# Merging order of a middle image's side steps: deadlines of one pace, or each with a correction of its own

## What is computed

```
x = x + conv3x3(gn(x))                          # layer 0
h = relu(bn1(nin(gn(x))))                       # layer 1, the dear one
y = mean over 4 directions d of mamba(h in direction d)
x = x + relu(bn2(nin2(y + h)))
x = x + gn(x) * gates(row and column means, two small mambas of 32 tokens)   # layer 2
x = x + post(circuit of 4 qubits(pre(gn(x))))   # layer 3
```

## Time and profile before

| | |
|---|---|
| median of 3 runs | 15168.12 us (15164.93 to 15168.78) |
| profiled execution | 15170.1 us, its span 15168.0 us |
| instructions | 190881 |
| granted TensorE clock, mean | 0.895 |
| PE, PEld busy | 85%, 54% |
| DVE, ACT, POOL busy | 89%, 61%, 90% |
| HBM | 207 GB/s over the span |

### The profile page before, as it was taken

The page is one execution under the profiler, slowest core; times in us unless marked ns, Lnnn a source line. Parts: engine busy times, 40 slices in busy tenths (PEclk is TensorE's granted clock), DMA queues, the critical chain, the costliest instruction groups (busy, mean ns, idle before and its releaser), DMA issues.

```text
span 15168.0 us, 190881 instructions
## 1 busy us (share of the span) xinstructions
PE 12942.3 (85%) x60700; PEld 8148.5 (54%) x60700; DVE 13545.8 (89%) x9901; ACT 9178.0 (61%) x10559; POOL 13633.9 (90%) x4234
## 2 busy tenths in 40 slices
PE   7888888888888888888888888888888888888886
PEld 4555555555555555555555555555555555555554
DVE  6988998889898898988899888999989899898996
ACT  4655665656666665665566665665656666566663
POOL 6998999989999898998989998999989899898996
PEclk8998998889899888989889998889988889888997
DMA  4655555555555555555555555555555555555653
GB/s 173 231 214 209 210 217 218 216 206 211 211 220 218 209 213 207 222 219 210 209 210 216 220 212 211 211 212 219 220 205 214 207 219 219 211 211 205 222 221 131
DMA packets 582385, 3200.85 MB, mean 211 GB/s; under 512 B 65875, under 2 KB 65883, under 8 KB 319075
## 3 DMA queue, kind: packets, MB, share of 16 engines
q1 hardware_dynamic: 581346, 3187.69, 56.6%
HBM read 3107.73 MB, written 29.36 MB: 207 GB/s over the span
## 4 chain that ended last, share of the span: by engine, by line
POOL 27%; issue 25%; PE 24%; DVE 17%; ACT 5%; DMA 1%; DVEq 1%; POOLq 0%; ACTq 0%; SPq 0%
POOL ring L884 18%; PE work L1387 13%; POOL ring L867 9%; DVE ring L1375 9%; PE y_acc L1402 6%; DVE slot L1364 4%; PE slot L1387 2%; PE y_acc L1387 2%; ACT ring L1041 1%; ACT L900 1%; DMA b_rows<-cb_rows_scratch 1%; DVE du L1163 1%; ACT stack L940 1%; ACT stack L936 0%; ACT yz L966 0%
## 5 line engine op out<-in xcount | busy, mean ns | idle before, releaser
L884 POOL TENSOR_TENSOR ring<-ring,c_rows 128x2048 f32<-128x2048 f32 x2048 | 9282.8, 4536 | 997.8 <-DVE ring L1375 993.7
L1375 DVE TENSOR_TENSOR_SCAN ring<-ring,slot 128x1024 f32<-128x1024 f32 x2304 | 5263.6, 2285 | 261.6 <-ACT ring L1041 38.2
L1402 PEld LDWEIGHTS y_acc<-wk,ring 128*128 128x128 f32 x32768 | 4252.3, 155 | 1880.0 <-issue 1021.7
L1402 PE MATMUL y_acc<-wk,ring 128*128 128x128 f32 x32768 | 4762.4, 297 | 489.7 <-POOL ring L884 406.8
L867 POOL TENSOR_TENSOR ring<-du,b_rows 128x1024 f32<-128x1024 f32 x1792 | 4236.3, 2365 | 286.6 <-PE y_acc L1402 211.0
L1375 DVE TENSOR_TENSOR_SCAN ring<-slot,ring 128x1024 f32<-128x1024 f32 x1792 | 4074.2, 2274 | 192.1 <-POOL ring L867 116.5
L1041 ACT ACTIVATE slot<-dt,a_neg 128x1024 f32<-128x1024 f32 x1792 | 1997.6, 1115 | 2784.0 <-DVE ring L1375 2777.6
L1364 DVE TENSOR_TENSOR slot<-du,slot 128x1024 f32<-128x1024 f32 x2304 | 2797.4, 1214 | 271.0 <-PE slot L1387 179.7
L1041 ACT ACTIVATE ring<-dt,a_neg 128x1024 f32<-128x1024 f32 x2304 | 2600.9, 1138 | 206.5 <-PE y_acc L1402 157.3
L1387 PE MATMUL work<-h_new,fused 128*128 128x512 f32 x4096 | 2160.0, 638 | 101.7 <-ACT dt L952 53.7
L1387 PE MATMUL slot<-stack,sel 96*128 96x512 bf16 x4608 | 1540.7, 419 | 719.4 <-DVE ring L1375 639.0
(11 more groups left out here) (173 smaller groups left out, 10050.2 us busy)
## 6 DMA issues: line engine op xcount, KB each, us to landing
c_rows<-cb_rows_scratch SPq DMA_DIRECT2D x2048, 1024.0 KB, 4.7
b_rows<-cb_rows_scratch SPq DMA_DIRECT2D x1792, 512.0 KB, 5.5
x_next<-in_x SPq DMA_DIRECT2D x32, 512.0 KB, 5.4
x_new<-x_next SPq DMA_DIRECT2D x32, 512.0 KB, 6.7
h_old<-h_new SPq DMA_DIRECT2D x32, 512.0 KB, 2.9
x_old<-x_new SPq DMA_DIRECT2D x32, 512.0 KB, 6.8
out<-x_old SPq DMA_DIRECT2D x32, 512.0 KB, 2.9
cb_rows_scratch<-stack SPq DMA_DIRECT2D x128, 96.0 KB
```

The costliest lines, as they stand in the source:

```text
L884: pool.tensor_tensor(pair, pair, c_rows[:, k % CB_BUFS, :, :], ALU.mult).then_inc(prod_ready, 1)
L1375: dve.tensor_tensor_scan(slot, a, b, 0.0, MUL, ADD).then_inc(scan_done, 1)
L1402: ins = pe.matmul(chunk(out_t, j), chunk(x, j), kc("ident"), is_transpose=True, start=start and j % (BANK // P) == 0, stop=stop, skip_grou ...
```

## The change

`lay` gets two arguments: the width of the window of choices, and a tuple of corrections for each stream. After the deadlines are worked out, each side step's due time is moved by half its correction, in us. For a middle image `image_plan` makes one plan only, with pace 3.22, a window of .2 and the table `SHIFTS`, six tuples with 160, 112, 44, 132, 12 and 19 whole numbers. The first and the last image are planned as before. The numbers of `SHIFTS` come from a search over the planner's timeline.

```
+PACE, WITHIN = 3.22, 0.2
+SHIFTS = [
+    (-230, -191, -308, 19, 76, 26, 91, -352, -323, -167, -317, 29, -260, -307, -343, 6, 629, 465, 26, -200, 249,
...
+    (234, -159, -25, -220, 215, -10, -88, 90, -220, -176, -61, 4, -296, -538, -351, -246, -773, -620, -647, -361,
...
+    (202, 74, 272, -168, -291, 21, -91, -294, -217, -279, -238, -551, -202, -15, 70, -208, -92, -254, 68, -551, -801,
...
+    (-98, -35, -51, 11, 209, 231, 79, 130, 240, -367, 126, -117, -215, -98, 6, 116, 4, -156, 233, -30, -30, -221,
...
+    (-56, -584, -160, -103, -67, -323, -425, -119, -322, -50, -399, -501),
+    (-37, -218, -63, 58, -50, -442, -130, -179, 46, 115, 186, 188, -63, -92, -80, 31, -89, -271, -240),
+]
...
-def lay(streams, kind, pace):
+def lay(streams, kind, pace, soon_within=SOON, shifts=()):
...
     want = deadlines(streams, by, pace)
+    for stream, shift in zip(streams, shifts):
+        for x, more in zip(stream, shift, strict=True):
+            want[x[0]] += .5 * more
...
-            soon = min(x[0] for x in choices) + SOON
+            soon = min(x[0] for x in choices) + soon_within
...
-    plans = [lay(streams, kind, pace) for pace in PACES]
+    plans = [lay(streams, kind, PACE, WITHIN, SHIFTS)] if kind == "mid" else [lay(streams, kind, pace) for pace in PACES]
```

## The result

The changed kernel takes 14903.99 us (median of 4 runs, 14892.47 to 14920.69), the kernel before 15166.6 in the runs beside it: 262.6 us less, ratio 0.9828 with a 95% interval of 0.9811 to 0.9845. The forecast was faster by 390 us, range 14480 to 15110. The direction held, the time lies in the range, and the gain was two thirds of what was forecast.

A forecast was written before the change was run, and what follows sets the result against it. DVE was taken as the tighter engine, its waits (36.7 us per image) as what a new order can remove. 30 images x 13 us = 390 us off 15168 gave 14778 us (14780.1 from the profiled execution), range 14480 to 15110.

The forecast's parts named there:

- What bounds it, and the floor: Middle image: DVE is the tighter engine, 430.7 us without waits; with 2.5% waiting the image would take 441.7 us.
- The stretch with 8.0 us per product: From 7750 to 7902 us POOL runs 19 products in 152 us; this stretch was to get shorter.
- The size of the gain: Middle images: 13 us per image taken as the middle, 30 x 13 = 390 us in all.
- half of 25.7: Middle image: 25.7 us is the gain at the floor, 0 the other end; the middle taken was 13 us.
- the fast stretch: From 7601 to 7750 us: 24 products, 6.2 us each, DVE waiting 2.5%, clock 0.95; shows what a good merge leaves.
- Which waits: DVE: side-step waits 20.8 us per image, seen by the search; unit waits 15.9, partly beyond any merge.
- The boundary: Pass boundary in the 27 us before 7601: ACT missed a `dt_proj` result for 15.24 us, DVE waited 2.90 for a decay.
- Table loads, SP, first and last image: ACT's table loads and SP's queue costed at nothing; first and last image keep their old plans.
- The clock: PE over the middle images: granted clock 0.90 before, forecast 0.90 or more, as a tighter merge gets a better clock.
- Rival 1: Middle images: clock returns with the merge, whole image runs like the fast stretch, 14397 us; chance 0.12.
- Rival 2: Planner's timeline: gain mostly its own; 1 to 8 us per image, 14930 to 15140 (0.15), or nothing, 15168 (0.06).
- Rival 3: Stretch 7750 to 7902: PE side matmuls end late, DVE's waits for PE grow 5.4 us per image, 15330 us; chance 0.09.

The follow-up runs named there:

- The pair of last runs: Kernel before, no corrections, `result` due at unit 84 instead of 88: 14924.42 us; the same with `take` at place 4 and the late drain: 14667.99 us.
- the pace alone: Changed kernel with pace 3.22 kept and all corrections zero: 15148.62 us, ratio 0.9985 against the kernel before.
- the three quarters: Changed kernel with all corrections at three quarters of their size: 15892.79 us, ratio 1.0475 against the kernel before.

## Why the prediction was right, and where it was not

- **What bounds it, and the floor.** Held. DVE's time outside its waits was 430.7 and is 431.0 us; all of the 9.7 us per image is waiting, and POOL's waits fell by as much, from 41.1 to (833.9 + 71.3 + 44.3) / 30 = 31.7. The stretch with 8.0 us per product, 7750 to 7902, is units 51 to 88; it did get shorter, units 48 to 88 from 166.1 to 159.5 us.
- **The size of the gain.** This is the term that was off: half of 25.7, 13 us per image, was taken, and 10.0 came in waits and 262.6 / 30 = 8.8 in the medians. That the time lies in a range of 630 us owes something to the width of the range. The half stood on the thought that a merge with 479 free numbers must come nearer to the fast stretch than a pace does. The pair of last runs shows the better reading: one place of 16 units held 13 to 14 us, the boundary 5, and each could be read off a table of lengths per eight units, which I had not made. I took the image in stretches of 150 us, in which the 69 us of units 80 to 96 do not stand out.
- **Which waits.** Wrong, and the right sum of all waits is here partly luck. The search was said to take the waits of side steps, 20.8 per image, and the units' own only in part. Side steps wait 21.5, units 5.3. The search did remove the wait of `result` (5.4 per image), but the boundary's `take` and others took its place, while the units' waits for spread, input and decay fell by two thirds.
- **The boundary.** It stood in the profile with 3 us of DVE's waiting, and I priced no loss there. In all, DVE waited 11.9 us in the 61 us of the two groups of units there, so there was something to win as well as to lose. The new plan put the last `take` ahead of the first scan, at 7.4 us of waiting. Where I wrote that a stall goes and what is late next, the cross-image step was missing.
- **Table loads, SP, first and last image.** Right at nothing: 1051 loads as before, `out` at most 5.9 us late, no wait of POOL on a transfer.
- **The clock.** Forecast 0.90 or more; the window shows 0.92 against 0.90. Rival 1, the full return, did not come (14397). But the clock is a larger part of the reasons than the sum had it: the removed matmuls made the kernel slower through it, and the one place that won went from 0.69 to 0.94. How much of its 13 us is the meeting of the jobs and how much the low clock isn't settled: in the kernel with `result` at unit 84 both changed at once, the images of the kernel before put some 3 us down to the clock (0.68 against 0.77), and the run with added spreads raised the clock by 0.08 and gained nothing.
- **Rival 2** (the planner's gain is its own). Partly true, as a statement on the planner: it was 4.4 us too long per image for before, 10.9 for the pace alone and 6.2 for the changed kernel, and 5.4 too short for the three quarters. So it had the sign of this change right (7.9 us promised, 9.7 found), and could have had it wrong for another.
- **Rival 3** (DVE's waits for PE grow). Fell: 610.8 us against 647.6, 20.4 per image.

## What to carry to other kernels

Before trusting or pricing a search over the order of work, cut the repeated unit of time into short pieces by a fixed event (here every eighth scan) and look for the few that are long; one place where three jobs of an engine meet, and one boundary between loop turns, held more here than 479 fitted numbers found, and three quarters of these numbers lost theirs at just such a place. A wait at a boundary goes only when every in-order queue that takes part in it is changed: moving its DVE step alone gave at most some 20 us, moving PE's drain as well 110 more. Corrections fitted together were good here only together, and what a new set gained on its timeline it didn't gain on the chip.

## What the runs showed that was not expected

Less work on PE made the kernel slower: with 15.6 us per image of D-term matmuls left out the granted clock fell from 0.92 to 0.89, and the image grew by 5.7 us. The opposite lever was weak: redundant spreads raised the clock from 0.919 to 0.928 and cost 89 us.

The images of one execution of the changed kernel are of two lengths, 457.4 or 460.8 us (the longer one 6 times in 28), with the same instructions in the same order. They part first at unit 4, by 1.5 us, and by unit 52 it is 4.8; the clock in units 0 to 8 is 0.90 in the long ones and 0.96 in the others. The images of the kernel before differ more, from 464.8 to 470.4, and yet its runs lie closer together: over 4 us beside the changed kernel, whose runs spread over 28, and over 19 in all the runs here. So images of unequal length don't explain the spread of the runs by themselves. That the granted clock's phase decides between the two lengths is my reading, and no run tested it.
